# Relative attention in 32-column strips: value products of four query tiles, one strip per tile, with one transpose in place of a fold

## The reference

```python
x = x + 0.5 * ffn(layernorm(x))
x = x + attn(layernorm(x))
x = x + 0.5 * ffn(layernorm(x))

# inside attn; q, k, v are (B, S, H, 16), p is the projected sinusoidal table
content = jnp.einsum('bihd,bjhd->bhij', q + u_bias, k)
pos = jnp.einsum('bihd,jhd->bhij', q + v_bias, p)
pos = _relative_shift(pos)
attn = jax.nn.softmax((content + pos) * scale, axis=-1)
head = jnp.einsum('bhij,bjhd->bihd', attn, v).reshape(B, S, Dm)
return head @ Wo + bo
```

## Time and profile before

| what | us |
|---|---|
| median of 3 runs (3958.25 to 4005.74) | 3978.27 |
| the profiled execution's own time | 3989.14 |
| its span, from the first to the last instruction | 3987.0 |
| first weight load of a content product, from the span's start | 511.4 |
| last weight load of one | 3733.9 |

### The profile page before, as it was taken

How to read it: one execution, slowest core, us unless ns; L and a number is a source line. 1 busy time by engine, 2 the same in 40 slices (tenths; PEclk the granted TensorE clock), 3 DMA queues, 4 the chain that set the end, 5 groups by cost and what they waited for, 6 DMA issues and landing times. The chain is left out here.

```text
span 3987.0 us, 86181 instructions
## 1 busy us (share of the span) xinstructions
PE 3510.2 (88%) x24380; PEld 1908.0 (48%) x24380; DVE 1830.6 (46%) x3584; ACT 2292.4 (57%) x3252; POOL 1262.1 (32%) x1224
## 2 busy tenths in 40 slices
PE   4666599999999999999999999999999999999867
PEld 3444344444444444444444444444444444444555
DVE  3555234444444444444444444444444444444354
ACT  1222156666666666666666666666666666666322
POOL 1111033333333333333333333333333333333200
PEclk7888789999999999999999999999999999999888
DMA  2333599999999999999999999999999999999543
GB/s 79 106 105 105 180 321 368 349 353 342 362 353 345 358 357 348 349 365 353 358 341 358 343 367 360 341 347 355 355 367 352 359 369 361 359 351 343 162 126 84
DMA packets 467979, 1221.59 MB, mean 306 GB/s; under 512 B 92144, under 2 KB 176624, under 8 KB 467952
## 3 DMA queue, kind: packets, MB, share of 16 engines
q1 hardware_dynamic: 467952, 1221.25, 89.8%
HBM read 624.38 MB, written 596.65 MB: 306 GB/s over the span
## 5 line engine op out<-in xcount | busy, mean ns | idle before, releaser
L719 DVE CUSTOM_DVE_ANT_0 at_pos_in<-at_ps_con,at_pos_in 128x1024 f32<-128x1024 f32 x1024 | 1254.0, 1225 | 1772.9 <-PE at_ps_con L607 1097.5
L756 POOL TENSOR_SCALAR at_pos_in<-at_pos_in,at_neg_max 128x1024 f32<-128x1024 f32 x1024 | 1145.6, 1119 | 2079.3 <-DVE at_neg_max L719 2079.3
L687 ACT ACTIVATE at_pos_out<-at_ps_pos 128x1024 f32<-128x1024 f32 x1024 | 1048.8, 1024 | 725.3 <-PE at_ps_pos L607 725.3
L696 ACT ACTIVATE at_prob<-at_ps_turn 128x512 f32<-128x512 f32 x2048 | 1116.4, 596 | 430.9 <-PE at_ps_turn L630 430.4
L607 PE MATMUL at_ps_con<-at_right,at_left 16*128 16x512 f32 x4096 | 1194.3, 659 | 192.4 <-DVE at_neg_max L719 188.6
L630 PEld LDWEIGHTS at_ps_turn<-keep_ident,at_pos_in 128*128 128x128 f32 x8192 | 935.2, 147 | 669.7 <-issue 464.8
L607 PE MATMUL at_ps_pos<-at_right,at_left 16*128 16x512 f32 x4096 | 1200.8, 663 | 43.4 <-DMA at_right<-scratch_pos_rows 35.5
L630 PE MATMUL at_ps_turn<-keep_ident,at_pos_in 128*128 128x128 f32 x8192 | 1157.1, 286 | 9.0
L642 PE MATMUL at_ps_pv<-at_prob,at_v_aug 128*32 128x512 f32 x4096 | 577.6, 638 | 0.7 <-issue 0.7
L607 PEld LDWEIGHTS at_ps_con<-at_right,at_left 16*128 16x128 f32 x4096 | 317.2, 188 | 398.1 <-issue 201.8
L653 PEld LDWEIGHTS at_ps_head<-keep_fold,at_head_T 128*128 128x128 f32 x2048 | 250.7, 193 | 198.2 <-DVE at_head_T L727 147.1
(11 more groups left out here) (80 smaller groups left out, 1308.6 us busy)
## 6 DMA issues: line engine op xcount, KB each, us to landing
scratch_scores<-at_pos_out SPq DMA_DIRECT2D x1024, 512.0 KB, 9.4
at_pos_in<-scratch_scores SPq DMA_DIRECT2D x1024, 512.0 KB, 9.4
at_left<-scratch_qk_rows SPq DMA_DIRECT2D x512, 64.0 KB, 5.8
scratch_qk_rows<-de_qk SPq DMA_DIRECT2D x48, 512.0 KB, 5.0
de_x<-in_L_attn_x_dram SPq DMA_DIRECT2D x16, 512.0 KB, 6.5
scratch_x<-de_x_bo SPq DMA_DIRECT2D x16, 512.0 KB, 3.0
scratch_values<-de_values SPq DMA_DIRECT2D x1, 8192.0 KB, 30.3
at_right<-scratch_pos_rows SPq DMA_DIRECT2D x256, 32.0 KB, 6.4
```

What stands on the lines that cost most here:

```text
L687: act.activation(pos_out[:, t.slot, :], ps_pos[:, :, :].rearrange("p a m -> p (a m)"), ACT.Copy)\
L696: act.activation(prob[t.t // QUAD % 2][:, 4 * n:4 * n + 4, k * P:(k + 1) * P], ps_turn[:, n, :].rearrange("p (j i) -> p j i", i=P), ACT.Exp)\
L719: dve.tensor_tensor_reduce(pos_in[:, t.slot, :], ps_con[:, :, :].rearrange("p a m -> p (a m)"), pos_in[:, t.slot, :], -SCALE, 3.0e38, ALU. ...
L756: pool.tensor_scalar(pos_in[:, t.slot, :], pos_in[:, t.slot, :], -1.0, neg_max[:, t.slot:t.slot + 1], ALU.mult, ALU.add).then_inc(shifted, 1)
```

## The change

Value products: strip g now belongs to query tile g of the quad. For each of the eight key tiles, four matmuls of 128 columns run, one in each strip, with the same values as weights in all four, and sum over all eight key tiles in PSUM. A half is four key tiles, so 16 matmuls of 128 columns where 4 of 512 stood. `ps_pv` and `head_T` shrink from 512 to 128 columns. As the sum is complete, the fold of four matmuls gives way to one transpose of `head_T` (`turn_heads`).

Turning and exponentials of tile t - 1 in step t become those of tile t - 2. The value products move from steps 1 and 2 to steps 2 and 3, the copy of the products from step 3 to step 0, the turning of heads and the division from step 0 to step 1, and the store of heads from step 5 to step 7 of a unit.

```diff
--- before.py
+++ after.py
@@ -462,11 +462,11 @@
         right = [sb(f"right{k}", [P, HALF]) for k in range(2)]
         v_in = [sb(f"v_in{k}", [P, P]) for k in range(2)]
         v_aug = [sb(f"v_aug{k}", [P, TILES, VW]) for k in range(2)]
-        head_T = sb("head_T", [P, QUAD * P])
+        head_T = sb("head_T", [P, P])
         inverse = sb("inverse", [P, QUAD])
         head = [sb(f"head{k}", [P, TILES * DH]) for k in range(2)]
         ps_pos, ps_con, ps_turn = (psum(n, [P, 2, 512]) for n in ("ps_pos", "ps_con", "ps_turn"))
-        ps_pv, ps_head = psum("ps_pv", [P, 512]), psum("ps_head", [P, QUAD, P])
+        ps_pv, ps_head = psum("ps_pv", [P, P]), psum("ps_head", [P, QUAD, VW])
 
         written, read = sems("written", RING), sems("read", RING)
         qv_in, qk_in, vals_in, head_out = (sems(n, 2) for n in ("qv_in", "qk_in", "vals_in", "head_out"))
@@ -585,7 +585,7 @@
                 if t % TILES == 1 and Tile(r, t - 1 + TILES).real():
                     load_qk(Tile(r, t - 1 + TILES))
                 done = Tile(r, t - TILES)
-                if t % TILES == 5 and done.real():
+                if t % TILES == 7 and done.real():
                     store_head(done)
 
             load_qv(Tile(0, 0))
@@ -637,22 +637,21 @@
                     pe.wait_ge(exped, t.count(2, 2 * QUAD))
                     if t.past(QUAD):
                         pe.wait_ge(pv_copied, t.quads())
-                for g in range(4):
-                    kt = 4 * half + g
-                    ins = pe.matmul(ps_pv[VW * g:VW * (g + 1), :], v_aug[t.side][:, kt, :],
-                                    prob[t.t // QUAD % 2][:, kt, :], start=(half == 0), stop=(half == 1))
+                for kt in range(TILES // 2 * half, TILES // 2 * (half + 1)):
+                    for g in range(QUAD):
+                        ins = pe.matmul(ps_pv[VW * g:VW * (g + 1), :], v_aug[t.side][:, kt, :],
+                                        prob[t.t // QUAD % 2][:, kt, g * P:(g + 1) * P],
+                                        start=(kt == 0), stop=(kt == TILES - 1))
                 if half == 1:
                     ins.then_inc(pv_mm, 1)
 
-            def fold(t):
+            def turn_heads(t):
 
                 pe.wait_ge(pv_copied, t.quads(1))
                 if t.past(QUAD):
                     pe.wait_ge(normed, t.quads())
-                for k in range(QUAD):
-                    ins = pe.matmul(ps_head[:, k, 0:VW], head_T[:, k * P:(k + 1) * P], keep["fold"][:, :],
-                                    start=True, stop=True)
-                ins.then_inc(head_mm, 1)
+                pe.transpose(ps_head[:, :, :].rearrange("p g v -> p (g v)"), head_T[:, :], keep["ident"][:, :])\
+                    .then_inc(head_mm, 1)
 
             def step(r, t):
                 if Tile(r, t).real():
@@ -663,14 +662,14 @@
                     strips(Tile(r, t), 0, ps_con, con_mm)
                 if Tile(r, t + LEAD).real():
                     strips(Tile(r, t + LEAD), 2 * STRIP, ps_pos, pos_mm)
-                if t % QUAD == 1 and Tile(r, t - 5).real():
-                    times_values(Tile(r, t - 5), 0)
                 if t % QUAD == 2 and Tile(r, t - 6).real():
-                    times_values(Tile(r, t - 6), 1)
-                if t % QUAD == 0 and Tile(r, t - 8).real():
-                    fold(Tile(r, t - 8))
-                if Tile(r, t - 1).real():
-                    turn(Tile(r, t - 1))
+                    times_values(Tile(r, t - 6), 0)
+                if t % QUAD == 3 and Tile(r, t - 7).real():
+                    times_values(Tile(r, t - 7), 1)
+                if t % QUAD == 1 and Tile(r, t - 9).real():
+                    turn_heads(Tile(r, t - 9))
+                if Tile(r, t - 2).real():
+                    turn(Tile(r, t - 2))
 
             pe.wait_ge(cleared, 1)
             for t in range(LEAD):
@@ -700,8 +699,8 @@
             def step(r, t):
                 if Tile(r, t + LEAD).real():
                     copy_positional(Tile(r, t + LEAD))
-                if Tile(r, t - 1).real():
-                    exponentials(Tile(r, t - 1))
+                if Tile(r, t - 2).real():
+                    exponentials(Tile(r, t - 2))
 
             for t in range(LEAD):
                 copy_positional(Tile(0, t))
@@ -742,10 +741,10 @@
             def step(r, t):
                 if Tile(r, t).real():
                     total(Tile(r, t))
-                if t % QUAD == 3 and Tile(r, t - 7).real():
-                    copy_products(Tile(r, t - 7))
                 if t % QUAD == 0 and Tile(r, t - 8).real():
-                    normalise(Tile(r, t - 8))
+                    copy_products(Tile(r, t - 8))
+                if t % QUAD == 1 and Tile(r, t - 9).real():
+                    normalise(Tile(r, t - 9))
 
             rounds(dve, step)
```

## The result

| | before | changed |
|---|---|---|
| median, us (20 runs each, taken together) | 3976.78 (3953.35 to 4012.72) | 4013.48 (3976.89 to 4042.74) |
| ratio to before, 95% interval | 1 | 1.0091 [1.0067, 1.0114] |
| the profiled execution's own time | 3989.14 | 4003.07 |
| tiles of the middle (992), us per tile | 3.145 | 3.166 |
| falls of the clock in them, time at the lower level | 30, 218 us | 35, 304 us |

The last four lines are counted from the records of the two traces. The change costs 0.9% where half a per cent of gain was forecast.

What follows compares the result with a forecast made beforehand. The prediction had TensorE and DMA bounding the kernel in turn, with clock falls. 3989 - 36 (DMA limit) + 15 (falls) + 3 (later end) = 3971, or 3960 us as median; range 3938 to 4000, wide 3895 to 4060.

Steps and rivals of the forecast that it cites:

- the case held likeliest: Whole kernel: nothing moves by 1%, time stays between 3938 and 4018 us; chance 0.48.
- The PE-paced quad: Four attention steps paced by TensorE: to fall from 11.90 to 11.64 us, 66 us over 256 quads.
- A half of the value products: Sixteen matmuls of 128 columns on TensorE: to take 0.99 to 1.05 us, against 0.99 before.
- The estimate of 2.6 us: Value products, per half: 32 pairs at the skill page's 0.081 us each; left out of the sum.
- The step that failed: Store of heads on SP, two steps later past four score transfers: said to wait for nothing, no cost in the sum.
- The new steps: Turning two steps behind: the attention phase ends one step later, plus 3 us, once.
- 15 falls at 1.0 us: Clock falls in the attention phase: 15 taken, each leaving 1.0 us after 2.2 us of slack, plus 15 us.
- DMA-limited 3.109 us per tile: Transfers in the 992 middle tiles: no faster than 3.109 us each, 3084 us in all, 36 less than before.
- signs that were to show the steps: Profile after: VectorE waits in half of tiles, full-clock stretches 49 to 50 us; 48 or less meant DMA limit misread.
- The second: Rival: clock falls more often, at strips of steps 0 and 1; 4020 to 4200 us; chance 0.10.
- The third: Rival: the value products' sixteen matmuls don't stream like four; 4095 us at 1.5 us per half; chance 0.11.
- The first, "PE's gain comes through": Rival: transfers keep 2.975 us per tile or clock falls nearly vanish; 3905 to 3938 us; chance 0.31.

Runs made afterwards that it cites:

- e1: Changed kernel with its steps put back (new products and transpose in the old steps, turning one step behind, store in step 5); ratio to before 0.9952.
- m1: The kernel before with one edit, the store of heads in step 7 in place of 5; ratio to before 1.0101.
- c2: The changed kernel, no edit, run a third time beside its variants on one chip; ratio to before 1.0101.
- n1: The changed kernel with one edit, the store of heads in step 3 of the next unit but one in place of step 7; ratio to before 0.9977.
- n4: New products in the old steps, with the store of heads in step 7 in place of 5; ratio to before 1.0064.
- e2: The kernel before, old products and fold kept, with all the moves of the change, store in step 7 included; ratio to before 1.0206.
- n3: The kernel before, old products and fold kept, on the new steps but with the store in step 3; ratio to before 1.0037.
- b3: The changed kernel with the unit's loads spread behind the write and read of steps 0 to 2, store still in step 7; ratio to before 0.9814.
- b1: New products and transpose in the old steps, with the unit's loads spread behind the write and read of steps 0 to 2; ratio to before 0.9843.
- n5: The changed kernel with the store in step 3 and the unit's loads spread over steps 0 to 2; ratio to before 0.9843.
- n6: n5 plus filler products of 224 and 160 columns, read by nobody, in steps 0 and 1; ratio to before 0.9795.
- k1: The changed kernel with the unit's loads spread late, two or three at a time in steps 1 to 4; ratio to before 0.9939.

## Why the prediction was wrong

The time of 4013 us lies in the wide range (3895 to 4060) and within 1% of before, the case held likeliest, but outside the forecast's own range (3938 to 4000) and on the other side of no change: 0.9% slower, with an interval clear of zero, where 0.5% faster was forecast. That the wide range held it is luck, as the sum below shows.

**What held.** The PE-paced quad was put at 11.64 us and takes 11.65. A half of the value products was put at 0.99 to 1.05 us and takes 1.01: 32 pairs, 0.032 us each. The estimate of 2.6 us from the Trainium skill ("TensorE: Matmul & The Clock Gate", section "Back-to-back issue gap") does not hold for pairs spread over four column strips. That estimate was left out of the sum, rightly. Step 1 with its transpose is as long as step 0 (2.68 and 2.76). VectorE's copy fell from 686 ns to 285 and moved nothing:

```profile
L726 DVE COPY at_head_T<-at_ps_pv 128x128 f32<-128x128 f32 x256 | 73.0, 285 | 3.6 <-PE at_ps_pv L642 3.6
```

The first experiment gives the new products and the transpose together -0.5%, the size of the whole forecast.

**The step that failed** is the last of the part on the moves: "The store of heads goes two steps later past four score transfers on SP, and waits for nothing there". It does wait for nothing. But it was costed at nothing because only its own wait was looked for. What it is put ahead of was not: the four unit loads, and behind them the write of the unit's first step and the read of tile 4. That pair already was the tightest. Counted from the trace of before, the row of tile 4 lands 0.26 us after the end of its content product (median) and that of tile 6 0.07 us after, where the other six tiles of a unit have 0.14 to 0.78 us to spare. The store pushes this write back by 0.77 us. The row then lands 0.38 us after (1.25 in the worst tenth, from 1.12): most of the push is won back, as the read then lands 8.6 us after its issue in place of 9.5. The change also took away the cover, for step 4 held the fold, 0.91 us of PE time. That accounts for where PE idles and where the clock falls, which e1 shows without any move of the store. The place of the store was changed alone in four pairs. On one chip it was worth 1.0% (m1 against before) and 1.2% (c2 against n1), across chips 1.1% (n4 against e1) and 1.7% (e2 against n3). Tile 6 comes later too (0.07 us late before, 0.24 now), but on one chip it is 0.52 us late in c2 and 0.53 in n1, so that is not the store's work. The new steps were put at 3 us, once, and cost 0.4% on the one chip where they were measured without the store (n3). That is the second term that was put too low, if its interval is taken at its word.

**Falls of the clock.** The sum had "15 falls at 1.0 us". There were 35, and a stretch with one takes 52.15 - 48.71 = 3.4 us more. With the DMA-limited 3.109 us per tile the sum gave 3084 + 15 = 3099 us for the 992 tiles. In the trace they come out at 992 x 48.71 / 16 + 35 x 3.4 = 3020 + 119 = 3139. The limit was 64 us too high, the falls 104 us too low. The two errors partly cancel, which is why the wide range held the time though two of its terms did not. Of the signs that were to show the steps, the data rate (353 GB/s, at most 360) and the landings (9.6 and 9.2 us) came as said. VectorE waits for rows in 390 of 1024 tiles, not in half, and stretches at full clock take 48.7 us, not 49 to 50: the limit was misread, if by less than the text's own mark of 48 us.

**The rivals.** The second (the clock falls more often, for want of work in steps 0 and 1) named the right direction and place of falls, but not the cause: its price was to set in at one and a half falls per 16 tiles, and 35 falls over 62 stretches are 0.56. The mean clock in the attention phase is 0.95, at its stated bound and not below. The third, products that do not stream, is excluded by the half of 1.01 us. The first, "PE's gain comes through", did not come true even with the store put right (n1, 0.9977). With the loads spread as well the change reaches it, 0.9814 in b3, on another chip.

**What stays open.** How much of the 0.4% for the new steps is real, and whether it comes from two light steps next to each other or from the late rows showing in them: the run with the products rotated mixed this with another place for the store. The rest of the way from the store's place to the time: the later row of tile 4 covers some 24 to 34 of 45 us. Why the changed kernel with spread loads (b3) comes out ahead of the new products in the old steps (b1): on their chip it is 15 us faster, run against run (3 to 28 us at 95%), though its light steps stand next to each other. And what the changed kernel itself takes on the slower chips: it was not run there, so b3, n5 and n6 are known against the kernel before alone.

## What to carry to other kernels

When a step with a DMA issue in it is moved, write down the order of all issues on that queue around the new place, and price the issue by what it is put ahead of, even if it waits for nothing: one issue that pushed the next back by 0.77 us per unit of 25 us cost one per cent here, as the transfer behind it had no slack. Work that is taken off an engine in front of a late transfer was its cover; look there first for where the gain goes, and for the clock to fall. An experiment that changes one number of the old kernel (m1) separates a side effect from the idea faster than any view of the changed kernel: here the views pointed at the steps behind tile 4, which idle as long with the store in its old place (e1).

## What the hardware showed that was not expected

- Sixteen float32 matmuls of 128 columns in four column strips take 1.01 us, four of 512 columns 0.99: four times as many loads and matmuls cost 2%.
- The clock fell from 2.4 to 1.2 GHz where PE had idled 1.74 us and then had strips and one transpose (changed kernel), and where it had idled 0.71 us and then had strips and the fold (before). Products of 384 columns in all per quad, read by nobody, cut the falls from 23 to 4 (n5 and n6).
- One chip takes 4% more than another for the same kernel (3978.92 and 4139.96 us). The early spread of loads (b1 to b3, n5, n6) ran only on slower chips, so its 2% is known for those. The late spread (k1) ran on the fast one and brought 0.6%.
